# Vision tower block on one core: gate columns made behind the first stage, bias rows split on GpSimd in the second stage, its loops in turns of six groups

## The reference, cut to what matters

```python
h = patches @ W_tok.T + b_tok                         # 768 -> 256
u = layernorm(h)
x = scan(x = A_bar * x + (u @ W_B.T + b_B) * dt)      # along the 196 tokens
h1 = h + x @ W_C.T + b_C + u @ W_D.T + b_D
x2 = layernorm(h1)
# attention over the 64 images, 4 heads of 64; then
y1 = ln(x2 + mha(x2), g1, be1)
gates = softmax(y1 @ wg); idx = argmax(gates)         # top-1 of 8 experts
# expert e: (t @ w1[e] + b1[e]) @ w2[e] + b2[e], at most S // 8 tokens each, in token order
out = h1 + ln(y1 + gate * expert(y1), g2, be2)
```

## Time and profile before

| what | us |
|---|---|
| median of 3 timed runs | 1288.45 (1282.59 to 1293.42) |
| the profiled execution | 1272.2 |
| its span, first to last instruction | 1270.4 |
| busy in the span: PE / DVE / POOL / ACT | 1126.9 / 1064.8 / 860.0 / 774.2 |
| mean granted TensorE clock | 0.970 |

### The profile page before, as it was taken

How to read it: one execution, slowest core, us unless ns; L and a number is a source line. 1 busy time by engine, 2 the same in 40 slices (tenths; PEclk the granted TensorE clock), 3 DMA queues, 4 the chain that set the end, 5 groups by cost and what they waited for, 6 DMA issues and landing times. The chain is left out here.

```text
span 1270.4 us, 36867 instructions
## 1 busy us (share of the span) xinstructions
PE 1126.9 (89%) x10938; PEld 1019.1 (80%) x10939; DVE 1064.8 (84%) x2843; ACT 774.2 (61%) x1714; POOL 860.0 (68%) x1153
## 2 busy tenths in 40 slices
PE   1999999999999999967999989989899974999994
PEld 0999999999999998966888888888888863666662
DVE  5589898989898999852788888888888887699997
ACT  3454646465656565523777777777777750688885
POOL 1565757576766676510688888888788884478887
PEclk9999999999999999978999999999999986999997
DMA  7444545454536364121233333333333325778872
GB/s 208 169 139 143 173 136 178 129 185 121 193 114 200 106 208 132 62 75 43 85 118 115 112 109 111 116 116 108 108 117 114 115 91 170 216 233 238 242 234 91
DMA packets 97308, 180.17 MB, mean 142 GB/s; under 512 B 12319, under 2 KB 62753, under 8 KB 96226
## 3 DMA queue, kind: packets, MB, share of 16 engines
q1 hardware_dynamic: 82500, 138.66, 36.3%
q0 software_dynamic: 13312, 39.75, 8.5%
q10 hardware_dynamic: 1440, 1.07, 0.3%
HBM read 112.69 MB, written 67.80 MB: 142 GB/s over the span
## 5 line engine op out<-in xcount | busy, mean ns | idle before, releaser
L532 POOL TENSOR_TENSOR xl<-xf,xh 128x512 fp32r<-128x512 f32 x141 | 192.9, 1397 | 176.0 <-ACT xh L447 176.0
L311 PE MATMUL ps_h<-wh,xh 128*128 128x256 f32 x588 | 166.4, 283 | 4.9 <-DVE xl L683 4.9
L311 PE MATMUL ps_h<-wl,xh 128*128 128x256 f32 x588 | 166.4, 283 | 0.0
L311 PE MATMUL ps_h<-wh,xl 128*128 128x256 f32 x588 | 166.1, 282 | 0.0
L1482 POOL DMA_INDIRECT out<-res,c_idx x106 | 123.8, 1168 | 43.0 <-issue 21.1
L1092 POOL DMA_INDIRECT bins<-rows,slot_i x98 | 101.2, 1033 | 60.1 <-POOL slot_i L1086 45.1
L1630 PE MATMUL c_ps_y<-w,yt 128*128 x424 | 118.1, 401 | 2.4 <-ACT c_py L1437 1.2
L311 PE MATMUL b<-x2h,wh 128*128 128x256 f32 x392 | 114.9, 293 | 4.9 <-issue 2.7
L311 PEld LDWEIGHTS ps_h<-wh,xh 128*128 128x128 f32 x588 | 112.3, 191 | 5.7 <-DVE xl L683 5.6
L577 DVE TENSOR_TENSOR_SCAN xs<-decay,xs,bu 128x256 f32<-128x256 f32 x96 | 101.7, 1100 | 13.3 <-ACT bu L459 8.3
L311 PEld LDWEIGHTS ps_h<-wh,xl 128*128 128x128 f32 x588 | 112.0, 190 | 0.0
(11 more groups left out here) (281 smaller groups left out, 4230.7 us busy)
## 6 DMA issues: line engine op xcount, KB each, us to landing
xf<-xt SPq DMA_DIRECT2D x49, 768.0 KB, 5.4
row<-bins SPq DMA_DIRECT2D x106, 257.5 KB, 3.7
h_dram<-h1b SPq DMA_DIRECT2D x49, 256.0 KB, 5.4
x_dram<-x2o SPq DMA_DIRECT2D x49, 256.0 KB, 5.6
x<-x_dram SPq DMA_DIRECT2D x98, 128.0 KB, 2.8
rows<-h_dram SPq DMA_DIRECT2D x98, 128.0 KB, 2.8
w1s<-w1t SPq DMA_DIRECT2D x8, 1024.0 KB, 7.4
w2s<-w SPq DMA_DIRECT2D x8, 516.0 KB, 5.9
```

What stands on the lines that cost most here:

```text
L311: last = nc.tensor.matmul(out_ps, a, b, start=(i == 0), stop=(i == len(terms) - 1))
L532: last = nc.gpsimd.tensor_tensor(xl[:, p, part], xf[:, p, part], xh[:, p, part].bitcast(F32), ALU.subtract)
```

## The change

- DVE's `fold_bias` keeps only the add; the four splitting instructions are gone from DVE. In the second stage POOL's step ends with `split_bias(k)`, for k from 0 to 47: part k % 6 of expert k // 6, one instruction of 2x256 in parts 0 to 4, none in part 5. [...]
- All gate work leaves the drain's steps. DVE does it behind its last step, PE behind the fold of the eighth expert (W_O is now transposed into ps_t), ACT behind its copy of w12.
- The second stage's loops on ACT, POOL, DVE and PE go from 8 straight steps and 20 turns of two to 6 straight steps and 7 turns of six. SP's loop stays.

```diff
             # ACT, first stage
-                    if isinstance(k.t, int) and k.c == NG + 2:
-                        act.wait_ge(turned, 1)
-                        nc.scalar.activation(wo_t[:], ps_f[:]...).then_inc(turned_out, 1)
...
-                    if isinstance(k.t, int) and k.c == NG + 3:
-                        act.wait_ge(wog_out, 1)
...
                 run(act, step, 0, NG + 5, 6, 42, FOLD)
                 act.wait_ge(fold_ps, NE)
                 nc.scalar.activation(w12[:, NE - 1, :], ps_f[:], ACT.Copy).then_inc(fold_out, 1)
+                act.wait_ge(turned, 1)
+                nc.scalar.activation(wo_t[:], ps_t[:]..., ACT.Copy).then_inc(turned_out, 1)
+                act.wait_ge(pre_in, 2)
+                nc.scalar.activation(gate_part(wh, W_QKV + 3 * D, QS), gg[:], ACT.Copy).then_inc(g_hi, 1)
+                act.wait_ge(wog_out, 1)
+                nc.scalar.activation(gate_part(wh, W_OUT + D, OS), wog[:], ACT.Copy).then_inc(g_hi, 1)
             # DVE, first stage, fold_bias
                         v.tensor_tensor(row, ps_fb[:], row, ALU.add).then_inc(fb_out, 1)
-                        v.tensor_copy(two, row).then_inc(fb_split, 1)
-                        v.tensor_tensor(row, row, two.bitcast(F32), ALU.subtract).then_inc(fb_split, 1)
-                        v.tensor_scalar(row, row, half[:, 1:2], None, ALU.mult).then_inc(fb_split, 1)
-                        v.scalar_tensor_tensor(two, two.bitcast(F32), half[:, 0:1], row, ALU.mult, ALU.add)...
...
                     fold_bias(k)
-                    if isinstance(k.t, int) and k.c == NG:
-                        gate_weights()
-                    if isinstance(k.t, int) and k.c == NG + 2:
-                        gate_low()
...
                 run(dve, step, 0, NG + 5, 6, 42, FOLD)
+                gate_weights()
+                dve.wait_ge(g_hi, 1)
+                v.tensor_tensor(gate_part(wl, W_QKV + 3 * D, QS), gg[:], ...).then_inc(g_lo, 1)
+                dve.wait_ge(wog_ps, 1)
+                v.tensor_copy(wog[:], ps_h[0]...).then_inc(wog_out, 1)
+                v.tensor_copy(sums[:], ps_h[0]...).then_inc(sums_out, 1)
                 dve.wait_ge(g_hi, 2)
             # PE, first stage
-                    if isinstance(k.t, int) and k.c == NG + 1:
-                        gate_first()
-                    if isinstance(k.t, int) and k.c == NG + 2:
-                        gate_second()
                 run(pe, step, 0, NG + 4, 6, 42, FOLD)
                 for c in range(FOLD):
                     fold(At(0, FOLD * (NE - 1) + c, FOLD))
+                # here the bodies of gate_first (into ps_t, waiting for h_done, u_lo, pre_in) and gate_second
             # POOL, second stage
+                def split_bias(k):
+                    if k.valid(FOLD * NE):
+                        e, part = k.turn(FOLD), k.slot(FOLD)
+                        row, two = (a[:, bass.ds(e, 1), :]... for a in (b12, b12s))
+                        if part > 0 and part < 5:
+                            wait(pool, split_b, e * 5 + part)
+                            apart(pool, passed["pool"])
+                        if part == 0:
+                            g.tensor_copy(two, row).then_inc(split_b, 1)
+                        elif part == 1:
+                            g.tensor_tensor(row, row, two.bitcast(F32), ALU.subtract).then_inc(split_b, 1)
+                        elif part == 2:
+                            g.tensor_tensor(row, row, half[:, 1:2].to_broadcast([2, D]), ALU.mult).then_inc(split_b, 1)
+                        elif part == 3:
+                            g.tensor_tensor(two, two.bitcast(F32), half[:, 0:1].to_broadcast([2, D]), ALU.mult)...
+                        elif part == 4:
+                            g.tensor_tensor(two, two.bitcast(F32), row, ALU.add).then_inc(split_b, 1)
...
                         if m.valid(NG):
                             stage(m)
+                    split_bias(k)
-                run(pool, step, 0, NG + 4, 8, 48)
+                run(pool, step, 0, NG + 4, 6, 48, FOLD)
             # and in the same way
-                run(act, step, 0, NG + 5, 8, 48)
+                run(act, step, 0, NG + 5, 6, 48, FOLD)
-                run(dve, step, 0, NG + 5, 8, 48)
+                run(dve, step, 0, NG + 5, 6, 48, FOLD)
-                run(pe, step, 0, NG + 4, 8, 48)
+                run(pe, step, 0, NG + 4, 6, 48, FOLD)
```

More of the change, by code:

```diff
@@ L365, in build @@
             h1b_done = a_sem("a_h1b_done")
-            w2_first, acc_done, fb_split = (a_sem(n) for n in ("w2_first_loaded", "fold_bias_sum", "fold_bias_split"))
+            w2_first, acc_done = (a_sem(n) for n in ("w2_first_loaded", "fold_bias_sum"))
             HALF = FK // 2 * D
@@ L519, in _ @@
                 nc.scalar.activation(w12[:, NE - 1, :], ps_f[:], ACT.Copy).then_inc(fold_out, 1)
+                act.wait_ge(turned, 1)
+                nc.scalar.activation(wo_t[:], ps_t[:].rearrange("p (t c) -> p t c", t=FT), ACT.Copy).then_inc(turned_out, 1)
+                act.wait_ge(pre_in, 2)
+                nc.scalar.activation(gate_part(wh, W_QKV + 3 * D, QS), gg[:], ACT.Copy).then_inc(g_hi, 1)
+                act.wait_ge(wog_out, 1)
+                nc.scalar.activation(gate_part(wh, W_OUT + D, OS), wog[:], ACT.Copy).then_inc(g_hi, 1)
             @blk.gpsimd
@@ L668, in fold_bias @@
                         row = b12[:, bass.ds(e, 1), :].rearrange("p a d -> p (a d)")
-                        two = b12s[:, bass.ds(e, 1), :].rearrange("p a d -> p (a d)")
                         v.tensor_tensor(row, ps_fb[:], row, ALU.add).then_inc(fb_out, 1)
-                        wait(dve, fb_out, e + 1)
-                        v.tensor_copy(two, row).then_inc(fb_split, 1)
-                        wait(dve, fb_split, e * 4 + 1)
-                        v.tensor_tensor(row, row, two.bitcast(F32), ALU.subtract).then_inc(fb_split, 1)
-                        wait(dve, fb_split, e * 4 + 2)
-                        v.tensor_scalar(row, row, half[:, 1:2], None, ALU.mult).then_inc(fb_split, 1)
-                        wait(dve, fb_split, e * 4 + 3)
-                        v.scalar_tensor_tensor(two, two.bitcast(F32), half[:, 0:1], row, ALU.mult,
-                                               ALU.add).then_inc(fb_split, 1)
                 for m in range(2):
@@ L852, in _ @@
                     fold(At(0, FOLD * (NE - 1) + c, FOLD))
+                pe.wait_ge(h_done, 2 * NG)
+                pe.wait_ge(u_lo, NG)
+                pe.wait_ge(pre_in, 3)
+                for t in range(FT):
+                    for i in range(FT):
+                        last = nc.tensor.transpose(ps_t[:, t * D + i * P:t * D + (i + 1) * P], wo[:, i, t * P:(t + 1) * P], ident[:])
+                last.then_inc(turned, 1)
+                pe.wait_ge(pre_in, 6)
+                mm, ps_g = nc.tensor.matmul, ps_h[0]
+                for t in range(FT):
+                    mm(ps_g[:, FT * NC:(FT + 1) * NC], ones_f[:], gg[:, t, :], start=(t == 0), stop=(t == FT - 1))
+                for t in range(FT):
+                    mm(ps_g[:, (FT + 2) * NC:(FT + 2) * NC + NE], spread[:, t, :], wg_sb[:, t, :], start=(t == 0), stop=(t == FT - 1))
+                for t in range(FT):
+                    mm(ps_g[:, (FT + 1) * NC:(FT + 2) * NC], spread[:, FT + t, :], gg[:, t, :], start=(t == 0), stop=(t == FT - 1))
+                pe.wait_ge(turned_out, 1)
+                for i in range(FT):
+                    for t in range(FT):
+                        last = mm(ps_g[:, i * NC:(i + 1) * NC], wo_t[:, t, i * P:(i + 1) * P], gg[:, t, :],
+                                  start=(t == 0), stop=(t == FT - 1))
+                last.then_inc(wog_ps, 1)
         patches.close()
@@ L912, in build @@
             row_ranks = sem("b_row_ranks")
+            split_b = sem("b_split_bias")
             h1_tok, x2_tok = (a.rearrange("(l j s t) d -> t j l s d", l=L, j=NG, s=2, t=2) for a in (h1_dram, x2_dram))
@@ L1029, in _ @@
                 g = nc.gpsimd
+                def split_bias(k):
+                    if k.valid(FOLD * NE):
+                        e, part = k.turn(FOLD), k.slot(FOLD)
+                        row, two = (a[:, bass.ds(e, 1), :].rearrange("p a d -> p (a d)") for a in (b12, b12s))
+                        if part > 0 and part < 5:
[8 more added lines that the diff above has]
+                        elif part == 3:
+                            g.tensor_tensor(two, two.bitcast(F32), half[:, 0:1].to_broadcast([2, D]), ALU.mult).then_inc(split_b, 1)
+                        elif part == 4:
+                            g.tensor_tensor(two, two.bitcast(F32), row, ALU.add).then_inc(split_b, 1)
                 def rstd(m):
```

38 lines of the change are left out of this document (4 added, 34 removed).

## The result

| | forecast | measured |
|---|---|---|
| changed kernel, median | 1291.2 us (1276 to 1311) | 1267.5 us (1266.3 to 1271.3, 4 runs) |
| before beside it | 1288.45 | 1287.5 us (1282.6 to 1293.4, 4 runs) |
| ratio | 1.002 | 0.9864 [0.9839, 0.9889] |
| profiled executions, span | 1270.4 to 1273.1 | 1270.4 to 1264.4 |

Faster by 1.4%, outside the range, and by 20.0 us, beyond the 12.9 from which the prediction counts a gain; it had given that a chance of 0.08. Between the two profiled executions the difference is only -6.0 us: SP's first load of the second stage comes 34.5 us earlier (forecast 22.1), from that load to POOL's last gate step it takes 27.6 us more (forecast 24.8), and from there to the end 0.9 more. So there are two misses: the first stage gained more, and the medians moved further apart than the profiled executions did.

A forecast was written before the change was run, and what follows sets the result against it. PE was taken to bound the first stage and POOL's full queue the second. First stage -22.1 us, second +24.8, third 0: net +2.7 on the median 1288.45 gave 1291.2 us, range 1276 to 1311.

The forecast's parts named there:

- so I count all twelve, 12.3 - 3.1 = 9.2 us: First-stage loop: without DVE's splits all twelve PE waits for ul vanish, 9.2 us gained (ends 4.6 and 9.2).
- The thirteenth, 3.1 us ... may still do so: 2.5: First stage after the seventh fold: PE's wait where scans run into POOL's split of x; 2.5 us gained (1.5 to 3.1).
- The drain: First stage's end: removing gate work and splits brings 14.0 us, new chain behind the fold costs 3.6; gain 10.4 (4 to 12).
- the 40 instructions: POOL's second-stage splits: 3 hidden, 37 count, 30 at 0.72 and 7 copies at 0.45; cost 24.8 us (7 to 46).
- The straight line between 20 and 512 elements: POOL's 2x256 split priced between 128x20 and 128x512 rows: 0.69 us, taken as 0.72; partition count does not enter.
- the pattern of five and one: POOL's second-stage step: near 10.1 us in five of six steps and 9.4 in the sixth.
- Rival A: POOL's second-stage split: each instruction makes one more collision with DVE, 17.8 us added, 1309.0 us; chance 0.16.
- Rival B: POOL's second-stage split is cheap, 0.18 to 0.25 us each, 7 to 9 us in all, 1274.4 us; chance 0.12.
- Loops of six: Second stage's turns of six instead of two: turn cost and spared collisions offset, 0 us (ends -9 and +4).
- Rival D: Second stage's long loop body: engines wait 2.8 us at each of 7 turns, 19.6 us more, 1310.8 us; chance 0.06.
- rival C: First stage keeps half its twelve waits and the drain gains nothing against its 3.6 us; +21.3, 1309.8 us; chance 0.08.
- so on their median the forecast is 1288.45 + 2.7: Whole kernel: net +2.7 us from the profiled execution added to the timed executions' median, giving 1291.2 us.

The follow-up runs named there:

- e10: Kernel before, bias splits as a DVE batch at the second stage's start, but two of four instructions per expert back on DVE in the first stage; 1252.16 us.
- e13: Kernel before, whole, plus one wait: POOL begins x low in the first stage only when DVE's scans are done; 1253.51 us, ratio 0.9845.
- e3: Changed kernel, but all experts' splits done by four DVE instructions of 2x2048 at the second stage's start, none on POOL; 1257.32 us, ratio 0.972.
- e4: Changed kernel again, unedited, on chip 1; 1270.38 us, ratio 0.9828.
- e14: Changed kernel with ACT's, DVE's and PE's second-stage loops in turns of two, only POOL's in turns of six; 1268.08 us, ratio 0.9949.
- e15: e3 unedited (DVE batch of splits, gates late, loops of six), on one chip with e14 and e16; 1238.54 us, ratio 0.9722.
- e16: DVE batch of splits at the second stage's start, gates late, loops of two, on one chip with e14 and e15; 1237.43 us, ratio 0.9712.
- e17: Changed kernel unedited on another chip (chip 5); 1267.2 us beside a kernel before of 1274.1, ratio 0.9943.
- e1: Kernel before with only the second stage's loops in turns of six, splits and gate columns as before; 1281.96 us, ratio 0.9906, on chip 1.
- e5: Kernel before again, unedited, in a second profiled execution, on chip 1; 1282.6 us.
- e11: e3 (DVE batch of splits, gates late, loops of six) with PE's second-stage loop alone in turns of two; 1237.09 us, ratio 0.9707.
- e18: Kernel before with gates late and x low held behind the scans, all splits still on DVE, loops of two; 1240.89 us, ratio 0.9739.
- e9: Kernel before, splits as a DVE batch at the second stage's start, but the first of four instructions back on DVE in the first stage; 1254.34 us.
- e6: Kernel before with all experts' splits as four DVE instructions at the second stage's start, gates early, loops of two; 1257.66 us.

## Why the prediction was wrong

Two steps failed: the size of PE's loss in the first stage (11.7 us counted for the loop and its end, 23.0 measured), and the basis from which the median was forecast. The other terms came near.

**First stage, the loop: mis-sized.** The step that failed is "so I count all twelve, 12.3 - 3.1 = 9.2 us". The displayed waits were taken for PE's whole loss. PE lost 2.5 to 2.7 us in each of six turns, 15.8 in all, which is beyond even the upper end of 9.2. Laid beside the changed kernel start by start, the turn from 131.27 shows where the rest was: its two displayed waits, 1.53 us, stand for 2.06 us of delay, since without a wait a matmul's modelled end lies behind the next one's start (records of 0.28 us, 0.12 us apart), and another 0.55 us go at the transposes of u with no displayed gap at all. A PE at 97.81 of 100 had in truth a turn 4.3% longer than without the splits. The measure that doesn't miss this is the turn from start to start, against a turn of PE's own work. The mechanism was half right: the splits made `ul` late. But the 0.97 us of the earlier trace rows were not simply what was left of 1.54 us of work: in such a step DVE loses 3.0 us by a collision which the splits set off. Half of the splits (e10) costs the loop nothing, and all of them cost it nothing with x low held back (e13).

**Its end: mis-sized.** "The thirteenth, 3.1 us ... may still do so: 2.5" named the collision, yet counted one wait. The steps of groups 41 to 48 gave 6.0 us; 4.6 of them are one step, 13.59 us for 8.98, whose displayed wait is 3.1. Another 1.2 us lay before the first transposes of u, where the profiled executions of all kernels scatter between 42.2 and 43.7.

**The drain: right.** 11.6 for 10.4. The clock stayed up, and from the last transpose of u to the end of the fold it gained 14.2 for 14.0; the gate work behind the fold added 2.6 us, 1.0 less than forecast (3.6, lower end 3.0).

**Second stage, the 40 instructions: near in size, by two errors of opposite sign.** 37 at about 0.58 us from start to start (0.69, 0.57 and 0.36) are 21.5 us, 3.3 less than the 24.8 forecast. e3 against e4 gives 23.9, the two profiles 27.6, e14 against e15 and e16 28 to 30. In the two profiles most of what is beyond 21.5 are the held copies, 13 more of 0.48 us, 6.2 us; the forecast had them under the loops of six and set them off against the turns. The straight line between 20 and 512 elements was good, and an instruction on 2 partitions costs what the line through rows of 128 gives. The step without a split was not 9.4 as forecast but 9.8 to 10.0, so the pattern of five and one was wrong: that step is the one with the loop's turn, and takes 9.9 in e15, where POOL splits nothing. Rival A, one held copy more for each split, did not come in its size: a copy is held in 38 of 49 steps of the changed kernel (40 in e4 and e14, 46 in e17) and in 36 of e15, though on chip 1 only in 16 of e3. Its counterargument was misread: of the straight steps before, not every one has a held copy, and the first of the earlier trace rows has none. Rival B is out by the 0.57 and 0.69.

**Loops of six: right at 0 on chip 8**, and as forecast: e15's steps are 9.34 to 9.44 with a held copy, one in six is 8.9 without, and the one with the turn is 9.9. On chip 1, e1 has 0.9906, though its profiled execution (1283.7) is no faster than e5's (1282.6); whether that ratio is a gain of the loops or the spread of the kernel before stays open. Rival D did not come; rival C neither.

**From the profiled execution to the median: wrong.** The step "so on their median the forecast is 1288.45 + 2.7" assumed that a difference found in one execution holds in the others. With the long rhythm (e5) POOL has room for part of the splits: its second stage goes from 455.7 to 473.8, +18.1, where the profiled one went from 445.2 to 473.3, +28.1. The medians are 20.0 us apart and the profiled executions 6.0; of the 14.0 between these, the rhythm gives 10. The remaining 4 are within the spread of the kernel before (1282 to 1302 us on chip 1), which I can't assign.

In sum, like with like: 1274.9 forecast for the profiled execution, 1266.3 measured, 8.6 too much; 12.4 too little gain in the first stage, 2.8 too little cost in the second, 1 in the third. For the median, the basis adds the rest. Whether this counts as faster hangs on where it is run: 0.986 beside a kernel before of 1287, 0.983 beside 1295, 0.994 beside 1274.

The best versions keep the gates late and leave POOL's second stage alone: e16, e11 and e15 at 1237 to 1239 us and e18 at 1241, 26 to 30 us below the changed kernel. The change's splitting on GpSimd gave back most of what its first stage won: 27.6 of 34.5 us.

## What to carry to other kernels

Size what an engine loses by its step from start to start against its own work, not by the sum of the displayed waits: short gaps are not in them. Where removing 1 us of one engine's work gives 2, look for a collision that the work pushes another instruction into; one wait that sets the order of the two may give the same with no work moved. An instruction moved to another engine is to be charged in full where that engine's queue is full, and before a difference is added to a median, check that the profiled execution is of that median's kind; here it was 10 us faster than all timed ones, and this was the sign.

## What was not expected of the hardware

- One program has two rhythms. In the second stage the same instructions take 443 to 445 us on three chips and 453 to 463 on a fourth (loops of two, no split on POOL), with equal durations of its instructions and other collisions (176 or 892 ns for `pos`). In the first stage's last steps it is 9.98 or 8.94 us, with and without one instruction of 0.28 us some steps before (e9 and e6).
- A DVE instruction of 128x2, 0.16 us, can take 1.06 us beside one POOL instruction of 128x512, and two scans of 1.40 take 3.50 beside three of them. In these rows the blocked one waits until POOL's instruction ends, however short it is itself, and POOL's third takes 1.68 us for 1.29.
- POOL's 2x256 costs what a straight line through 128x20 and 128x512 gives (0.69 us from start to start with two full inputs), 0.57 with one input of stride 0, and 0.36 for a copy. The forecast's estimate for the copy, 0.4 us by the Trainium skill (GPSIMD Engine Reference, section 3.1), agrees.
